# Three expert weight loads, issued from ScalarE's queue at the start of the program

## The chip, the cores and the metric

One core of a Trainium2 chip (trn2) runs the whole program; the seven other cores are idle. The metric is the device time of one execution in microseconds (us). All data is fp32 unless said otherwise. The engines are TensorE (PE), VectorE (DVE), ScalarE (ACT), GpSimd (POOL) and SyncE (SP), each with an instruction queue of its own that it works through in order; 16 DMA engines move the data.

## What is computed

The reference is a "macaron" block over 8 x 512 tokens of width 128 (4096 tokens in all): a mixture-of-experts feed-forward, attention, and the same feed-forward again, with the same weights.

```python
x = x + 0.5 * ffn(layernorm(x), router_w, w_gate, w_up, w_down, ws_gate_up, ws_down)
x = x + attn(layernorm(x), wq, bq, ..., gamma, beta)      # 16 heads of width 8, layernorm inside
x = x + 0.5 * ffn(layernorm(x), ...)

def ffn(x):                       # T = 4096 tokens as given; 64 experts, 8 per token, 64 slots per expert
    probs = softmax(x @ router_w.T)
    topk_w, topk_ids = top_k(probs, 8); topk_w /= sum(topk_w)
    # an expert takes its first 64 tokens, later ones are dropped
    h = silu(xb @ w_gate) * (xb @ w_up)       # per expert: [64,128] @ [128,96], twice
    y = h @ w_down                            # per expert: [64,96] @ [96,128]
    return segment_sum(y * topk_w) + (silu(sg) * su) @ ws_down    # plus one shared expert
```

The three expert weights are `w_gate` and `w_up` [64, 128, 96] and `w_down` [64, 96, 128], each 64 x 128 x 96 x 4 bytes = 3.146 MB, 9.44 MB together. The input tokens are 4096 x 128 x 4 bytes = 2.10 MB.

## The kernel before

The program is one block with a hand-written instruction stream for each engine. Every order between engines is made by semaphores, and `wait(engine, semaphore, count)` holds that engine's queue at this point. Both feed-forwards use the same function `ffn(f)` on each engine, with `f.p` 0 for the first and 1 for the second.

All state stays on chip: `x_sb` holds the 4096 tokens as 32 tiles of 128 tokens, `wg_sb`, `wu_sb` and `wd_sb` hold all expert weights. They are loaded once, and both feed-forwards read them.

The start of the program, in the order of its work:

- SP (lines 322 to 348) issues four loads of 8 token tiles each (L326), the router weight `rw_sb` (L327), two shared-expert weights (L328, L329), the attention's weights and biases (L337 to L347), and then the first third, five DMAs, of the fill of `routed_sums` in HBM with zeros (`zero_sums(0, 0, 3)`, L335). Then it enters `ffn`.
- DVE takes statistics of each tile as the tokens come (L925), waits for the transposed router weight (L927), and computes mean and variance (L659, L661).
- ACT's first instruction is the square root of the variance plus epsilon (L937, in `ffn`), with the load of its table before it; DVE takes the reciprocal (L666). This `rstd` releases everything after it.
- The routing runs over 8 groups of 4 tiles. POOL normalises a group (`normalise`, L503 and L507) into one of two buffers `xn_sb`; it may overwrite a buffer only when SP's store of it into `dispatch_rows` (L355) has landed. PE transposes it (L1064), ACT copies it out of PSUM (L942, L943), PE forms the router's logits (L1069), and DVE takes the 8 best of each token (L688 to L714). SP stores the groups and their weights (L355, L359) and, after the first weights, a second third of the zero fill.
- DVE then makes the list of 64 tokens of each expert in one chain of `max` and `match_replace` (L735, L737), while PE, ACT and POOL compute the shared expert.
- In this time SP issues the last third of the zero fill and then the three expert loads (L374), each counting `s_wexp` up by 16.
- When the list is ready (L752), POOL gathers the rows of two experts per indirect DMA (L550). PE waits for `s_wexp` to be 48 (L1117) and then runs the experts in 16 steps of four (L1125, L1150, L1136); DVE weights the results (L774), POOL adds them into `routed_sums` (L563).

Nothing else reads `s_wexp`, and nothing writes the three weight tiles again. ACT issues no DMA in this kernel.

Of the kernel before, what the change touches and what calls it, by code (L numbers as in the profile page):

```python
# [14 lines left out]
def macaron_kernel(nc, x_in, wq, bq, wk, bk, wv, bv, wo, bo, gamma, beta,  # L15
# [9 lines left out]
    T = B * S  # L25
    NT = T // P
    E, _, F = w_gate.shape
    K8, C = 8, 64
    NP2 = E // 2
# [26 lines left out]
    with ExitStack() as ctx:  # L56
        def sb(name, shape, dt=F32):
            return ctx.enter_context(nc.sbuf_tensor(name, shape, dt))

        def sem(name):  # L60
            return ctx.enter_context(nc.semaphore(name))

        def wait(eng, s, value):

            if isinstance(s, Event):
                s, value = s.sem, value + s.base
            if isinstance(value, int) and value <= 0:
                return
            eng.wait_ge(s, value)
# [30 lines left out]
        wg_sb = sb("wg_sb", [P, E, F])  # L100
        wu_sb = sb("wu_sb", [P, E, F])
        wd_sb = sb("wd_sb", [F, E, D])
# [105 lines left out]
        s_wexp = sem("experts_loaded")  # L208
# [114 lines left out]
        def _(sp):  # L323
# [8 lines left out]
            def zero_sums(p, part=0, parts=1):  # L332
                z = acc_dram[p].rearrange("(c p r) d -> c p (r d)", p=P, r=10)
                for c in range(part, z.shape[0], parts):
                    sp.dma_start(z[c], zeros[:]).then_inc(s_acc0[p], 16)  # L335
# [14 lines left out]
            def ffn(f):  # L350
                rows = xw_dram[f.p].rearrange("(i p) c -> p i c", p=P)

                def store(g, r):
                    wait(sp, f.xn, g + 1)
                    sp.dma_start(rows[:, bass.ds(g * GT, GT), 0:D], xn_sb[:, r, :, :]).then_inc(f.xns[r].sem, 16)  # L355

                def store_w(g, r):
                    wait(sp, f.w, g + 1)
                    sp.dma_start(rows[:, bass.ds(g * GT, GT), D:XW], w_r[r].rearrange("p (i e) -> p i e", i=GT))\  # L359
                      .then_inc(f.ws[r].sem, 16)  # L360
                store(0, 0)
                store(1, 1)
                store_w(0, 0)
                if f.p == 0:
                    zero_sums(0, 1, 3)
                with sp.Fori(1, NG // 2) as i:
                    for r in range(2):
                        store(2 * i + r, r)
                        store_w(2 * i + (r - 1), 1 - r)
                store_w(NG - 1, 1)  # L370
                if f.p == 0:
                    zero_sums(0, 2, 3)
                    for w, t in ((w_gate, wg_sb), (w_up, wu_sb), (w_down, wd_sb)):
                        sp.dma_start(t[:], w.rearrange("e k n -> k e n")).then_inc(s_wexp, 16)  # L374

                wait(sp, f.shx, NG)
                wait(sp, f.sca[0], 16 * (NP2 // 2))
                wait(sp, f.sca[1], 16 * (NP2 // 2))
                accs = acc_dram[f.p].rearrange("(a t) d -> a t d", a=NACC)[:, 0:T, :].rearrange("a (i p) d -> a p i d", p=P)

                def load(g, r):
                    wait(sp, f.acca, g - 1)
                    for a in range(NACC):
                        sp.dma_start(acc_r[r * NACC + a].rearrange("p (i d) -> p i d", i=GT),  # L384
                                     accs[a, :, bass.ds(g * GT, GT), :]).then_inc(f.accl[r].sem, 16)
                def store_out(g):
                    wait(sp, f.acca, g + 1)
                    sp.dma_start(out_rows.rearrange("(i p) d -> p i d", p=P)[:, bass.ds(g * GT, GT), :],
                                 x_sb[:, bass.ds(g * GT, GT), :]).then_inc(s_out, 16)
                load(0, 0)  # L390
                load(1, 1)
                with sp.Fori(1, NG // 2) as i:
                    for r in range(2):
                        load(2 * i + r, r)
                        if f.p == 1:
                            store_out(2 * i + (r - 2))
                if f.p == 1:
                    store_out(NG - 2)
                    store_out(NG - 1)
                    sp.wait_ge(s_out, 16 * NG)  # L400

            def attention():
# [68 lines left out]
                ctx_load(NT - 1, (NT - 1) % NBUF)  # L471

            ffn(ffns[0])
            attention()
            ffn(ffns[1])


# [454 lines left out]

        @block.scalar
        def _(act):
            def ffn(f):
                wait(act, f.ve, 1)
                act.activation(rstd[:], rstd[:], ACT.Sqrt).then_inc(f.sd.sem, 1)  # L937

                def route(g, r):
                    wait(act, f.xtp, g + 1)  # L940
                    wait(act, f.lg, g - 1)
                    act.activation(xT_r[r], bank[r][:], ACT.Copy).then_inc(f.xts.sem, 1)  # L942
                    act.activation(xT_all[:, bass.ds(g * (GT * P), GT * P)], bank[r][:], ACT.Copy).then_inc(f.xts.sem, 1)  # L943
                    wait(act, f.d, GT * (g + 1))
                    wait(act, f.w, g - 1)
                    act.activation(e_r[r], d_r[r], ACT.Exp).then_inc(f.ex.sem, 1)
                route(0, 0)
                route(1, 1)
                with act.Fori(1, NG // 2) as i:
                    for r in range(2):  # L950
                        route(2 * i + r, r)
                for b in range(4):
                    wait(act, f.ktp, b + 1)
                    act.activation(KT[:, b * 512:(b + 1) * 512], bank[4 + b][:], ACT.Copy).then_inc(f.kts.sem, 1)  # L954

                def shared_up(g, r):
                    wait(act, f.shp, g + 1)
                    wait(act, f.shh, g - 1)
                    act.activation(shs[r][0:F, :], bank[r][0:F, :], ACT.Silu).then_inc(f.shs.sem, 1)
                    act.activation(shu[r][0:F, :], bank[2 + r][0:F, :], ACT.Copy).then_inc(f.shc.sem, 1)  # L960

                def shared_out(g, r):
                    wait(act, f.sho, g + 1)
                    wait(act, f.shx, g - 1)
                    act.activation(shy[r], bank[4 + r][:], ACT.Copy, scale=0.5).then_inc(f.shy.sem, 1)
                shared_up(0, 0)
                shared_up(1, 1)
                shared_out(0, 0)
                with act.Fori(1, NG // 2) as i:
                    for r in range(2):  # L970
                        shared_up(2 * i + r, r)
                        shared_out(2 * i + (r - 1), 1 - r)
                shared_out(NG - 1, 1)

                for q in range(NP2 // 2):
                    r = q % 2
                    wait(act, f.gtp, q + 1)
                    wait(act, f.gu, q - 1)
                    act.activation(gT[r], bank[r][:, 0:2 * P], ACT.Copy).then_inc(f.gts.sem, 1)  # L979
                    wait(act, f.gu, q + 1)  # L980
                    wait(act, f.hid, q - 1)
                    act.activation(sil[r][0:F, :], bank[2 + r][0:F, 0:4 * C], ACT.Silu).then_inc(f.sil.sem, 1)  # L982

            def attention():
# [63 lines left out]
                for t in range(NT):  # L1048
                    z = z_sb[:, t * P:(t + 1) * P]
                    act.activation(z, z, ACT.Identity, scale=rstdz[:, t:t + 1], bias=negm[:, t:t + 1]).then_inc(a_zn, 1)  # L1050

            ffn(ffns[0])
            attention()
            ffn(ffns[1])


# [256 lines left out]
```

## Time and profile before

| | us |
|---|---|
| median of 3 runs | 985.01 |
| lowest, highest | 984.28, 988.32 |
| the profiled execution | 990.85 |
| its span, first to last instruction | 989.0 |

| engine | busy us | share of the span |
|---|---|---|
| PE | 681.7 | 69% |
| DVE | 682.7 | 69% |
| ACT | 420.0 | 42% |
| POOL | 409.3 | 41% |

By stage, from the span's start: tokens and statistics until about 15 us, routing until 65 us, the experts' token lists until 108 us, the expert steps until about 210 us, then the sum, attention, and the second feed-forward from 739 us on. In the rows below, SPq is SP's queue: the time of a `DMA_DIRECT2D` there is how long the issuing instruction held the queue, not how long the data took. "Idle before" in brackets is how long the engine had been idle, and what ended it. L12 is line 12 of the kernel.

### The profile page before, as it was taken

Reading aid. Unit: us, or ns where it says so; the run is one execution under the profiler, and the core shown is the slowest. Engines: PE = TensorE matmul, PEld = TensorE weight load, DVE = VectorE, ACT = ScalarE, POOL = GpSimd, SP = SyncE. Lnnn points to the kernel's source line nnn. Section 1 sums busy time; section 2 is a strip of 40 time slices with the busy share of each in tenths; the row PEclk is TensorE's granted clock in tenths of the full one; section 3 lists DMA queues with packets and bytes.
Section 4 is the critical chain, followed back from the end, with each engine's and each line's share of the span. In section 5 each row is a group of like instructions: output and inputs, shape, how many; then the busy total and the mean of one; then the engine's idle time right before and its main releaser. Section 6 shows DMA issues by size and latency. Waiting matters only on the chain.

```text
span 989.0 us, 16170 instructions
## 1 busy us (share of the span) xinstructions
PE 681.7 (69%) x4579; PEld 335.1 (34%) x4579; DVE 682.7 (69%) x1396; ACT 420.0 (42%) x885; POOL 409.3 (41%) x492
## 2 busy tenths in 40 slices
PE   2576397600389999999999999999605682886200
PEld 1443285500123333333333333332104441775100
DVE  5899332358797888888888888887276995322345
ACT  2234011000037777777777777777653350111000
POOL 2417478786622233332223333210045173788722
PEclk9998555555589999999999999999955595555555
DMA  7549733347759964444545444451102200233377
GB/s 233 202 151 292 128 51 52 47 68 207 146 74 253 240 124 91 82 88 91 96 86 93 84 85 89 93 96 34 38 0 70 59 1 23 55 51 53 32 208 216
DMA packets 247426, 103.42 MB, mean 105 GB/s; under 512 B 150713, under 2 KB 238937, under 8 KB 247385
## 3 DMA queue, kind: packets, MB, share of 16 engines
q1 hardware_dynamic: 235096, 92.44, 40.4%
q0 software_dynamic: 12288, 10.49, 7.4%
q8 instruction: 19, 0.31, 0.1%
q14 instruction: 23, 0.18, 0.1%
HBM read 58.33 MB, written 44.30 MB: 104 GB/s over the span
## 4 chain that ended last, share of the span: by engine, by line
PE 42%; DVE 22%; issue 12%; DMA 10%; POOL 6%; ACT 3%; SPq 3%; another core or an unknown queue 1%; DVEq 0%; ACTq 0%; POOLq 0%
PE psum L1223 13%; PE psum L1232 13%; PE psum L1210 10%; DMA routed_sums<-arena 5%; DVE arena L735 4%; DVE arena L737 4%; POOL arena L550 4%; DMA arena<-routed_sums 3%; DVE x_sb L789 2%; ACT arena L1022 2%; DVE arena L835 2%; PE psum L1177 2%; POOL routed_sums L563 1%; SPq L384 1%
## 5 line engine op out<-in xcount | busy, mean ns | idle before, releaser
L835 DVE TENSOR_REDUCE arena<-psum 128x2 f32<-128x1024 f32 x256 | 308.7, 1220 | 51.4 <-PE psum L1210 48.2
L1022 ACT ACTIVATE arena<-psum 128x512 f32<-128x512 f32 x512 | 282.0, 600 | 114.0 <-PE psum L1223 112.6
L1210 PE MATMUL psum<-arena 126*128 126x512 bf16 x512 | 196.8, 391 | 9.7 <-DMA arena<-qk_parts 5.0
L1223 PE MATMUL psum<-arena 128*128 128x512 bf16 x512 | 195.6, 385 | 7.3 <-ACT arena L1022 3.3
L1232 PE MATMUL psum<-arena 128*32 128x512 f32 x1024 | 136.2, 604 | 0.3
L622 POOL CAST arena<-arena 128x256 bf16<-128x256 f32 x32 | 12.7, 398 | 262.6 <-issue 260.1
L774 DVE TENSOR_SCALAR arena<-psum,arena 64x128 f32<-64x128 f32 x128 | 44.7, 350 | 110.2 <-DMA routed_sums<-arena 97.7
L563 POOL DMA_INDIRECT routed_sums<-arena x64 | 101.0, 1578 | 29.3 <-DVE arena L774 15.2
L1223 PEld LDWEIGHTS psum<-arena 128*128 128x128 bf16 x512 | 50.4, 100 | 149.2 <-ACT arena L1022 121.7
L550 POOL DMA_INDIRECT arena<-dispatch_rows,arena x64 | 62.8, 981 | 45.6 <-DVE arena L752 26.7
L789 DVE TENSOR_TENSOR x_sb<-x_sb,arena 128x512 f32<-128x512 f32 (+1 forms) x48 | 48.7, 1015 | 35.9 <-DMA arena<-routed_sums 34.0
L982 ACT ACTIVATE arena<-psum 96x256 f32<-96x256 f32 x32 | 12.2, 381 | 139.1 <-PE psum L1150 124.7
L1210 PEld LDWEIGHTS psum<-arena 126*128 126x128 bf16 x512 | 49.3, 99 | 42.5 <-DVE arena L835 14.8
L1136 PE MATMUL psum<-wd_sb,arena 96*64 96x128 f32 x256 | 35.9, 435 | 34.3 <-DVE arena L759 34.3
L1150 PE MATMUL psum<-arena,wg_sb 128*96 128x64 f32 x256 | 49.4, 374 | 7.6 <-ACT arena L979 5.9
L1069 PE MATMUL psum<-rwT,arena 128*128 128x64 f32 x128 | 31.4, 427 | 29.4 <-ACT arena L942 29.4
L1150 PEld LDWEIGHTS psum<-arena,wg_sb 128*96 128x96 f32 x256 | 43.4, 275 | 18.4 <-issue 10.7
L1150 PE MATMUL psum<-arena,wu_sb 128*96 128x64 f32 x256 | 47.6, 367 | 0.0
L1150 PEld LDWEIGHTS psum<-arena,wu_sb 128*96 128x96 f32 x256 | 44.8, 280 | 0.0
L1172 PE MATMUL psum<-ident,arena 128*128 128x128 f32 x32 | 10.9, 341 | 48.7 <-POOL arena L607 40.5
L1064 PE MATMUL psum<-ident,xn_sb 128*128 128x128 f32 x64 | 17.1, 424 | 37.7 <-POOL xn_sb L507 37.7
L735 DVE MAX8 arena<-arena 128x8 f32<-128x2048 f32 (+1 forms) x32 | 41.3, 1290 | 1.8 <-ACT arena L954 0.8
(120 smaller groups left out, 979.5 us busy)
## 6 DMA issues: line engine op xcount, KB each, us to landing
routed_sums<-zeros SPq DMA_DIRECT2D x26, 640.0 KB, 5.5
arena<-routed_sums SPq DMA_DIRECT2D x64, 256.0 KB, 4.3
arena<-qk_parts SPq DMA_DIRECT2D x128, 96.0 KB
ctx<-arena SPq DMA_DIRECT2D x32, 256.0 KB, 2.0
qk_parts<-arena SPq DMA_DIRECT2D x32, 192.0 KB, 3.7
dispatch_rows<-xn_sb SPq DMA_DIRECT2D x16, 256.0 KB, 2.3
arena<-qk_parts SPq DMA_DIRECT2D x64, 64.0 KB
arena<-ctx SPq DMA_DIRECT2D x64, 64.0 KB, 2.3
```

The costliest lines, as they stand in the source:

```text
L550: pool.indirect_dma_start(out=gat[k % NGB], out_offset=None, in_=xw_dram[f.p], in_offset=bass.IndirectOffsetOnAxis(ap=gidx[:, k:k + 1], ax ...
L563: pool.indirect_dma_start(out=acc_dram[f.p], in_=y_r[k % NYB], in_offset=None, out_offset=bass.IndirectOffsetOnAxis(ap=sidx[:, k:k + 1], a ...
L735: link(dve.max(dst[:, c:c + 8], src))
L737: link(dve.match_replace(src, dst[:, c:c + 8], src, 0.0))
L774: dve.tensor_scalar(y_r[k % NYB][rows, :], bank[4 + r][rows, j * D:(j + 1) * D], gat[k % NGB][rows, col:col + 1], None, ALU.mult).then_inc ...
L789: ins = dve.tensor_tensor(xs, xs, src, ALU.add)
L835: dve.tensor_reduce(mx_r[r % 2][:, 2 * p:2 * p + 2], src, X, ALU.max).then_inc(a_mx, 1)
L1022: act.activation(p_r[tau % NPB], bank[4 + tau % 2][:, :], ACT.Exp, scale=SCALE).then_inc(a_P, 1)
L1150: ins = pe.matmul(bank[2 + r][0:F, off + m * C:off + (m + 1) * C], w[:, 4 * q + m, :], gT[r][:, m * C:(m + 1) * C], start=True, stop=True)
L1210: ins = pe.matmul(bank[tau % 4][:, :], heads(q_st[r], rows, g)[:, qt * P:(qt + 1) * P], heads(k_st[r], rows, g), start=True, stop=True)
L1223: pe.matmul(bank[4 + tau % 2][:, :], keys, heads(q_st[r], rows, g), start=True, stop=True)\
L1232: ins = pe.matmul(bank[6][32 * g:32 * g + 32, :], v_r[r][:, g, kt, :], p_r[(4 * kt + g) % NPB], start=(kt == 0), stop=(kt == 3), tile_posi ...
```

## The change

The three loads leave SP's stream and become the first instructions of ACT's. Tiles, sources, semaphore and counts are the same.

```diff
@@ sync: ffn(f), after store_w(NG - 1, 1) @@
                 if f.p == 0:
                     zero_sums(0, 2, 3)
-                    for w, t in ((w_gate, wg_sb), (w_up, wu_sb), (w_down, wd_sb)):
-                        sp.dma_start(t[:], w.rearrange("e k n -> k e n")).then_inc(s_wexp, 16)
@@ scalar @@
         @block.scalar
         def _(act):
+            for w, t in ((w_gate, wg_sb), (w_up, wu_sb), (w_down, wd_sb)):
+                act.dma_start(t[:], w.rearrange("e k n -> k e n")).then_inc(s_wexp, 16)
+
             def ffn(f):
                 wait(act, f.ve, 1)
```

## Rows read from the trace of the kernel before

**Rows 1.** The timeline, first 19 us: start us, us, engine, line, operation [idle before].

```profile
0.76 1.28 ACT L937 ACT_TABLE_LOAD   x1 [0.76 <-PEq L1303]
0.76 3.71 SPq L326 DMA_DIRECT2D x_sb<-in_L_attn_x  x4
...
10.09 1.65 DVE L925 BATCH_NORM_STATS2 stats<-x_sb 128x6 f32<-128x128 f32 x8 [0.23 <-DMA x_sb<-in_L_attn_x]
...
11.91 2.21 DVE L659 BATCH_NORM_AGGREGATE mv<-stats 128x2 f32<-128x6 f32 x32
...
14.32 3.80 SPq L335 DMA_DIRECT2D routed_sums<-zeros  x5
14.36 0.23 ACT L937 ACTIVATE rstd<-rstd 128x32 f32<-128x32 f32 x1 [12.32 <-DVE rstd L661]
14.62 0.35 DVE L666 RECIPROCAL rstd<-rstd 128x32 f32<-128x32 f32 x1 [0.30 <-ACT rstd L937]
```

**Rows 2.** Timeline of SP's queue, 60 to 100 us, the expert loads.

```profile
69.01 1.04 SPq L374 DMA_DIRECT2D wg_sb<-in_L_ffn_w_gate  x1
70.50 11.91 SPq L374 DMA_DIRECT2D wu_sb<-in_L_ffn_w_up  x1
82.46 9.52 SPq L374 DMA_DIRECT2D wd_sb<-in_L_ffn_w_down  x1
```

**Rows 3.** DMA issues over the span: count, KB each, us from issue to landing.

```profile
wd_sb<-in_L_ffn_w_down SPq DMA_DIRECT2D x1, 3072.0 KB, 30.6
...
wu_sb<-in_L_ffn_w_up SPq DMA_DIRECT2D x1, 0.4 KB, 26.2
```

**Rows 4.** DMA view of 6 to 8 us: tokens alone.

```profile
DMA packets 1166, 0.59 MB, mean 294 GB/s; under 512 B 16, under 2 KB 1166, under 8 KB 1166
## 3 DMA queue, kind: packets, MB, share of 16 engines
q1 hardware_dynamic: 1166, 0.59, 118.4%
```

**Rows 5.** DMA view of 77 to 80 us: gate and up weights alone.

```profile
DMA packets 644, 0.99 MB, mean 330 GB/s; under 512 B 0, under 2 KB 644, under 8 KB 644
```

**Rows 6.** DMA view of 98 to 101 us: down weights alone.

```profile
DMA packets 988, 0.51 MB, mean 169 GB/s; under 512 B 0, under 2 KB 988, under 8 KB 988
```

**Rows 7.** DMA issues between 14 and 20 us: count, KB, us to landing.

```profile
routed_sums<-zeros SPq DMA_DIRECT2D x5, 640.0 KB, 7.8
dispatch_rows<-xn_sb SPq DMA_DIRECT2D x2, 256.0 KB, 8.5
```

**Rows 8.** Chain of waits, 16 to 67 us: start us, us, what.

```profile
18.16 8.72 DMA dispatch_rows<-xn_sb
...
27.27 1.05 POOL xn_sb L503
...
65.35 2.31 DVE arena L735
```

**Rows 9.** The timeline of the second feed-forward, the same stage.

```profile
741.68 0.35 DVE L666 RECIPROCAL rstd<-rstd 128x32 f32<-128x32 f32 x1 [0.30 <-ACT rstd L937]
...
744.36 2.50 SPq L355 DMA_DIRECT2D dispatch_rows<-xn_sb  x2
...
747.01 1.04 POOL L503 TENSOR_TENSOR xn_sb<-x_sb,mv 128x512 f32 x1 [0.56 <-DMA dispatch_rows<-xn_sb]
...
788.32 2.29 DVE L735 MAX8 arena<-arena 128x8 f32<-128x2048 f32 x1 [0.38 <-ACT arena L954]
```

**Rows 10.** The timeline, 108 to 115 us, from the finished list to the first expert matmul.

```profile
108.19 0.19 DVE L752 TENSOR_TENSOR arena<-arena 128x32 uint32<-128x32 f32 x1
...
113.44 0.66 PE L1125 MATMUL psum<-ident,arena 128*128 128x128 f32 x2 [6.73 <-DMA arena<-dispatch_rows,arena]
...
114.57 1.54 PE L1150 MATMUL psum<-arena,wg_sb 128*96 128x64 f32 x8 [0.47 <-ACT arena L979]
```

**Rows 11.** The timeline of the second feed-forward, the same place.

```profile
831.14 0.19 DVE L752 TENSOR_TENSOR arena<-arena 128x32 uint32<-128x32 f32 x1
...
837.21 1.54 PE L1150 MATMUL psum<-arena,wg_sb 128*96 128x64 f32 x8 [0.47 <-ACT arena L979]
```

## The prediction, made blind

> **What bounds the kernel at the two ends of the change.** I read first the chain of waits, to see what the stages around the two places hang on, then the timeline of both places, then the DMA view of short stretches in which one kind of transfer runs alone, and last the same stages of the second feed-forward, which has no expert loads and no zero fill beside it.
>
> At the start everything hangs on the tokens. The last eight statistics begin at 10.09 us, released by the token load; the aggregation follows, ACT takes the square root at 14.36, and `rstd` is ready at 14.62 + 0.35 = 14.97 us [rows 1]. ACT had then been idle for 12.32 us, and before that held only a table load of 1.28 us at 0.76. The 16 DMA engines have nothing to spare while the tokens come: 118.4% by the view's own measure, where packets overlap, at 294 GB/s [rows 4].
>
> The next wait on the path is a DMA again: the store of the first normalised group is issued at 18.16 and POOL gets its buffer back only at 27.27, after 9.11 us, since the five zero fills stand before it in the same queue [rows 1, 7, 8]. In the second feed-forward that step takes 747.01 - 744.36 = 2.65 us [rows 9]. From `rstd` to the first `MAX8` of the lists the first feed-forward needs 65.35 - 14.97 = 50.4 us, the second 788.32 - 742.03 = 46.3 [rows 1, 8, 9]. So some 4.1 us of the first one are owed to this traffic.
>
> At the other end, the expert loads are in flight from 69 us; the last lands at 82.46 + 30.6 = 113.1 us [rows 2, 3]. That looks late, since PE begins at 113.44. But what released PE is the first gather, and from L752 to the first expert matmul it is 114.57 - 108.19 = 6.38 us here and 837.21 - 831.14 = 6.07 us in the second feed-forward, without any load [rows 10, 11].
>
> **What is removed.** Three issues leave SP's queue (22.5 us of it), behind which SP has nothing due until the expert steps are over. The loads leave the stage of the lists, where DVE works from its own tiles. The gain is the difference just read: 0.3 us. It can't be much more, because PE would next wait for the gather, whose time without loads is the 6.07.
>
> **What is added: ACT's queue.** The three issues are copied from SP: 1.04, 11.91 and 9.52 us [rows 2]. The second and third are long because each returns only when the load before it is nearly through: the third returned at 82.46 + 9.52 = 91.98, and the up weights landed at 70.50 + 26.2 = 96.7, 4.7 us later [rows 2, 3]. So ACT is free when gate and up are almost moved. Both are 6.29 MB, at 0.330 MB per us [rows 5] 19.1 us. Beside nothing else ACT would be free about 18 us after the first packet, at some 20 us. The trace has no DMA issued from ACT; I take SP's behaviour for it. The bounds: held for nothing but three short issues (about 3 x 1.04 us, free at 4), or held until everything that shares the engines has passed too (below, 35).
>
> **What is added: the tokens share the engines.** Tokens alone need 2.10 MB / 0.294 = 7.1 us [rows 4]. How two queues divide the engines is not shown, so from both sides. If they take turns by packets: a token packet is 0.59 MB / 1166 = 0.5 KB, 583 pass per us, which is 27 ns on each of 16 engines; a gate or up packet is 0.99 MB / 644 = 1.5 KB, 215 pass per us, 75 ns [rows 4, 5]. One of each takes 102 ns, so 157 token packets pass per us and the 4096 need 26.1 us: 19.0 more. If they take turns by bytes, 4.2 MB at about 0.31 take 13.5 us: 6.4 more. The best case is no delay.
>
> The Trainium skill, "DMA: Bandwidth & Descriptors", section "Queues, rings and completion order", says that each DMA engine goes round its queues by whole packets. No run here has shown it yet; by that rule it is the 26.1 us, by equal bytes the 13.5, and it is one reason for the small chance that I give to the mild case below.
>
> *By packets:* the last tokens come 19.0 us later, and `rstd` at 14.97 + 19.0 = 34.0. In these 26 us gate and up have also passed (26.1 x 157 x 1.5 KB = 6.3 MB), so ACT is free at about 28, and with its table load (1.28, hidden before, now behind the issues) and the square root and reciprocal at 30. The tokens are the later of the two. Delay 19.0 us. SP's small loads follow the tokens in order, so the zero fill stands before the first store again, sharing with the down weights (0.51 MB in 3 us, slow ones [rows 6]); I give back 1 us of the 4.1. Sum: +18.0.
>
> *By bytes:* the tokens are done 6.4 us later and no longer decide. ACT's turn comes after 20 + 7.1 (tokens) = 27, and now SP gets to its five zero fills before that: 3.28 MB, which needed some 8 us [rows 7]. ACT is free at 35, `rstd` is ready at 35 + 1.28 + 0.23 + 0.35 = 37. Delay 22. But the zero fills are through when the first store is issued, so up to 4.1 us come back. Sum: +18.
>
> Both ways of sharing lead to the same place, so I take +18 at the start and -0.3 at the end. Other stages only shift: routing runs at DVE's pace, and the rest of the down weights (some 18 us at 0.169 MB per us [rows 6]) lies beside it with small stores between. The profiled execution would go from 990.85 to about 1008.5, with a span of about 1007. It lies 5.8 us above the median of the runs, and I carry the same difference to the median: 985.0 + 18 = 1003.
>
> **The rivals.**
>
> *The queues hinder each other when issuing.* If the expert issues hold not only ACT but also what turns SP's requests into packets, the four token loads are let in one by one between the expert loads. With the last token load behind all three, the tokens are complete after 19.1 + 3.146 / 0.169 = 18.6 + 7.1 = 44.8 us instead of 7.1: delay 37.7, less the 0.3 and nothing given back, because the zero fill again comes late: 1022. For it: SP's own issues already lengthen when the queue is full (four token issues 3.71 us [rows 1]). Against: nothing in the trace has two issuers of this kind. It decides only if the last token load gets behind the down weights; behind gate and up alone it is 26 us, the forecast. The Trainium skill, "Perfetto Trace Analysis", section "DMA Instruction — HWDGE (DVE, Sync)", says that the descriptor generator is locked for one issuer until it has generated all descriptors. That is this rival, and no row of before can show it.
>
> *The mild case.* ACT is not held, or the engines carry both streams at nearly full rate. Then only the 6.4 us of equal bytes remain, or 20 + 1.9 - 15 = 7 us of ACT. The buffer that comes back at 27.27 regardless [rows 8] hides 2.7 to 4.1 us of that: +3 to +4, 988.5. For it: the loads alone stay below 400 GB/s. Against: the DMA share is over 100% already [rows 4].
>
> *Not slower.* A delay of `rstd` under about 2.7 us disappears wholly in the wait for the zero fill that ends at 27.27. That needs the tokens to be nearly through before expert packets come in numbers, and ACT free before 14 us. Then it is 985.0 - 0.3 = 984.7. It decides at 2.7 us. Against: the first expert issue goes out at 0.76 us, together with the first token issue, and the second and third can't return early unless ACT's queue behaves otherwise than SP's [rows 2].
>
> A real gain has no place: the end of the loads is worth 0.3 us. That the edit does nothing is excluded, since it issues 9.44 MB before the tokens are there.
>
> **How the numbers follow.** Forecast (+14 to +24) 0.62; mutual hindrance 0.20; mild 0.12; not slower 0.06. The likeliest is 1003. The range of 8 in 10: from the mild case at 989, which leaves out the not-slower case and half of the mild one, up to 1024 to hold the hindrance. Of the chance outside, some 0.12 lies below and 0.06 above. One measurement of this kernel tells about 0.5% (4.9 us) from no change. Within it lie the not-slower case and about half of the mild one: same 0.10; faster 0.02; slower 0.88.
>
> **What would show it.** In the profile after: ACT's queue begins with three issues, the second and third over 9 us each, and its table load comes after them, near 28 to 35 us. The last statistics begin near 29 us by packets and near 17 by bytes. `rstd` is ready at 34 to 37. The wait for the first store is shorter than 9.1 us. From L752 to the first expert matmul it is about 6.1 us, and every later stage has its old length. Token statistics beginning after 40 us show the hindrance; ACT's square root before 20 us shows the mild case. I am wrong if ACT's issues are short, if the tokens keep their 10 us, or if later stages change their length.

## The result, and the profile after

| | before | after |
|---|---|---|
| median us | 984.64 (4 runs) | 1007.16 (4 runs) |
| lowest, highest | 983.41, 988.32 | 1005.38, 1008.33 |
| ratio, 95% interval | 1 | 1.0222 (1.0201 to 1.0244) |
| profiled execution | 990.85 | 1005.38 |
| its span | 989.0 | 1003.5 |

The change makes the kernel 22.5 us slower (19.8 to 24.0 by the interval of the ratio); a median of 1003 was forecast. ACT's square root is at line 938 now, DVE's reciprocal at L664, POOL's normalising at L501 and L505, the first `MAX8` of the lists at L733, their end at L750.

The timeline after, its first 32 us and the place where the lists begin (start us, us, engine, line, operation [idle before]):

```profile
0.76 10.10 SPq L326 DMA_DIRECT2D x_sb<-in_L_attn_x  x4
0.81 0.91 ACTq L934 DMA_DIRECT2D wg_sb<-in_L_ffn_w_gate  x1
...
2.18 13.37 ACTq L934 DMA_DIRECT2D wu_sb<-in_L_ffn_w_up  x1
...
15.59 14.54 ACTq L934 DMA_DIRECT2D wd_sb<-in_L_ffn_w_down  x1
15.76 0.76 SPq L328 DMA_DIRECT2D wsgu_sb<-in_L_ffn_ws_gate_up  x1
...
24.21 1.65 DVE L923 BATCH_NORM_STATS2 stats<-x_sb 128x6 f32<-128x128 f32 x8 [2.81 <-DMA x_sb<-in_L_attn_x]
...
28.27 0.18 DVE L659 TENSOR_SCALAR rstd<-mv 128x32 f32<-128x32 f32 x1
30.16 1.28 ACT L938 ACT_TABLE_LOAD   x1 [28.00 <-issue]
31.45 0.23 ACT L938 ACTIVATE rstd<-rstd 128x32 f32<-128x32 f32 x1
31.71 0.35 DVE L664 RECIPROCAL rstd<-rstd 128x32 f32<-128x32 f32 x1 [3.27 <-ACT rstd L938]
...
86.96 2.29 DVE L733 MAX8 arena<-arena 128x8 f32<-128x2048 f32 x1
```

Against [rows 1]: the last statistics begin at 24.21 instead of 10.09. The variance is ready at 28.45, and ACT's table load begins only at 30.16, behind its three issues. `rstd` is ready at 31.71 + 0.35 = 32.06 instead of 14.97: 17.1 us. Of these 14.1 are the tokens and 3.0 what ACT adds, 1.28 of them its table load, which lay hidden before [rows 1].

The two queues beside each other, in the DMA view of 10 to 12 us after:

```profile
DMA packets 618, 0.63 MB, mean 316 GB/s; under 512 B 0, under 2 KB 618, under 8 KB 618
## 3 DMA queue, kind: packets, MB, share of 16 engines
q10 hardware_dynamic: 309, 0.47, 78.1%
q1 hardware_dynamic: 309, 0.16, 30.8%
```

q10 is the new queue, ACT's. Both move 309 packets, ACT's three times as large: here the turn goes by packets. The tokens pass at 155 per us instead of 583 [rows 4].

It doesn't go so all the time. By the same view q1 had moved 1013 packets by 4 us, before q10 came in numbers; from 4 to 6 us q10 moved 406 packets and q1 only 32; from 7 to 16 us they took equal turns; and from 16 to 18 us, when the gate weights were nearly through, q1 moved 992 and q10 only 78.

Then the routing. The chain of waits after:

```profile
34.41 9.06 DMA dispatch_rows<-xn_sb
43.86 1.05 POOL xn_sb L501
...
46.30 13.91 DMA dispatch_rows<-xn_sb
60.55 1.04 POOL xn_sb L501
```

Before, one store was waited for like this, 9.11 us [rows 8]; now there are two: 43.86 - 34.41 = 9.4 and 60.55 - 46.30 = 14.2 us. From `rstd` to the first list step it is 86.96 - 32.06 = 54.9 us instead of 50.4. Together the lists begin 86.96 - 65.35 = 21.6 us later [rows 8]. The timeline after, at the end of the lists:

```profile
129.78 0.19 DVE L750 TENSOR_TENSOR arena<-arena 128x32 uint32<-128x32 f32 x1
...
136.02 1.54 PE L1151 MATMUL psum<-arena,wg_sb 128*96 128x64 f32 x8 [0.47 <-ACT arena L980]
```

That is 6.24 us, 0.14 less than in [rows 10].

From the first expert matmul to the end the profile after needs 867.5 us, and the ten other kernels that were profiled (below) 865.5 to 870.1; so the later stages keep their length. The profiled execution of before is the one that stands out, with 874.4 us: 4.9 of the excess lie between its first expert matmul and its first weighted result (13.0 us, in all the other profiles 8.1), and why is not shown. That is why the spans differ by only 14.5 us and the medians by 22.5. The shift of 21.6 us at the lists is the better measure of the change; less the 0.14 it is 21.5, inside the interval.

### The profile page after: what moved, and what is told of

It reads as the page before. It is cut to its first block, busy times and chain, and to the rows that moved or that the text cites. A ratio compares the mean times of both kernels' runs of the same rounds, so it can differ in the third digit from the quotient of the medians.

```text
span 1003.5 us, 16109 instructions
## 1 busy us (share of the span) xinstructions
PE 676.2 (67%) x4518; PEld 335.1 (33%) x4579; DVE 681.5 (68%) x1396; ACT 420.4 (42%) x887; POOL 408.5 (41%) x492
## 3 DMA queue, kind: packets, MB, share of 16 engines
q10 hardware_dynamic: 10288, 9.44, 3.4%
## 4 chain that ended last, share of the span: by engine, by line
PE 38%; DVE 20%; issue 12%; DMA 11%; POOL 8%; ACT 5%; ACTq 3%; SPq 1%; DVEq 0%; POOLq 0%
PE psum L1233 13%; PE psum L1224 11%; PE psum L1211 9%; DMA routed_sums<-arena 5%; POOL arena L548 5%; ACT arena L1023 4%; DVE arena L733 4%; DVE arena L735 4%; DMA arena<-routed_sums 3%; ACTq L934 3%; DVE x_sb L787 2%; DMA dispatch_rows<-xn_sb 2%; DVE arena L833 2%; POOL routed_sums L561 1%; SPq L382 1%
## 5 line engine op out<-in xcount | busy, mean ns | idle before, releaser
L1224 PE MATMUL psum<-arena 128*128 128x512 bf16 x451 | 172.4, 385 | 7.1 <-ACT arena L1023 3.3
L561 POOL DMA_INDIRECT routed_sums<-arena x64 | 100.9, 1577 | 24.5 <-issue 14.8
L1224 PEld LDWEIGHTS psum<-arena 128*128 128x128 bf16 x512 | 50.4, 100 | 149.1 <-ACT arena L1023 121.7
L548 POOL DMA_INDIRECT arena<-dispatch_rows,arena x64 | 62.6, 977 | 45.0 <-DVE arena L750 26.1
L787 DVE TENSOR_TENSOR x_sb<-x_sb,arena 128x512 f32<-128x512 f32 (+1 forms) x48 | 48.7, 1015 | 33.9 <-DMA arena<-routed_sums 32.1
L1211 PEld LDWEIGHTS psum<-arena 126*128 126x128 bf16 x512 | 49.3, 99 | 42.5 <-DVE arena L833 14.5
L501 POOL TENSOR_TENSOR xn_sb<-x_sb,mv 128x512 f32 (+1 forms) x16 | 17.0, 1065 | 68.3 <-DMA dispatch_rows<-xn_sb 33.8
```

The costliest lines, as they stand in the source:

```text
L548: pool.indirect_dma_start(out=gat[k % NGB], out_offset=None, in_=xw_dram[f.p], in_offset=bass.IndirectOffsetOnAxis(ap=gidx[:, k:k + 1], ax ...
L561: pool.indirect_dma_start(out=acc_dram[f.p], in_=y_r[k % NYB], in_offset=None, out_offset=bass.IndirectOffsetOnAxis(ap=sidx[:, k:k + 1], a ...
L787: ins = dve.tensor_tensor(xs, xs, src, ALU.add)
L1211: ins = pe.matmul(bank[tau % 4][:, :], heads(q_st[r], rows, g)[:, qt * P:(qt + 1) * P], heads(k_st[r], rows, g), start=True, stop=True)
L1224: pe.matmul(bank[4 + tau % 2][:, :], keys, heads(q_st[r], rows, g), start=True, stop=True)\
```

## Experiments

My theory after the result had three terms: the tokens take turns with the expert packets (14.1 us), ACT stands behind its own issues (3.0 us), and the stores of the routing wait longer (4.5 us). The rival for each was that one of the others is the whole cause. "List" is the start of the list steps; the kernel before has 65.35.

| kernel | median us | ratio (95%) | last statistics | `rstd` | first store, us | list |
|---|---|---|---|---|---|---|
| before | 985 | 1 | 10.1 | 15.0 | 9.1 | 65.4 |
| after | 1007.2 | 1.0222 (1.0201 to 1.0244) | 24.2 | 32.1 | 9.4 | 87.0 |
| tokens first | 1013.3 | 1.0289 (1.0275 to 1.0303) | 10.2 | 44.1 | 9.6 | 93.9 |
| gate only | 993.5 | 1.0090 (1.0076 to 1.0104) | 21.1 | 26.1 | 7.4 | 74.3 |
| fill late | 1000.9 | 1.0174 (1.0158 to 1.0190) | 24.1 | 32.0 | 9.4 | 81.3 |
| two ahead | 1000.3 | 1.0156 (1.0142 to 1.0170) | 24.5 | 29.4 | 10.7 | 80.8 |
| down after the square root | 1003.8 | 1.0186 (1.0171 to 1.0201) | 24.5 | 29.4 | 12.0 | 84.0 |
| two ahead, fill late | 994.9 | 1.0095 (1.0080 to 1.0110) | 24.7 | 29.6 | 2.7 | 76.5 |
| fill spread | 984.8 | 0.9995 (0.9983 to 1.0006) | 10.2 | 15.1 | 2.7 | 62.5 |
| fill spread, gate on ACT | 982.8 | 0.9989 (0.9977 to 1.0002) | 10.2 | 15.1 | 2.7 | 63.5 |
| ACT at the old time | 999.4 | 1.0137 (1.0119 to 1.0155) | 10.2 | 15.1 | 9.1 | 65.4 |
| down first | 1011.7 | 1.0278 (1.0263 to 1.0292) | 19.9 | 44.5 | 8.3 | 93.1 |

"First store" runs from the issue of the first store to POOL's next use of a buffer. "Last statistics" is the start of the last eight; for "gate only" it is the middle of a row of sixteen (19.42, 3.43 us long). The ratios are to the runs of before on the same chip (984.4 to 985.0 us). One more kernel was planned, with the square root of the first feed-forward taken by DVE, so that `rstd` doesn't wait for ACT's queue; it gave no time. "Two ahead" and "down after the square root" answer its question.

### Tokens first

```diff
         def _(act):
+            for c in range(4):
+                act.wait_ge(s_x[c], 16)
             for w, t in ((w_gate, wg_sb), (w_up, wu_sb), (w_down, wd_sb)):
                 act.dma_start(...)
```

> ACT waits for all four token loads before it issues the three expert loads, so the tokens have the DMA engines to themselves. Theory 'the issues hold ACT': the tokens land near 10 us as before, but ACT's second and third issue return only when gate and up are nearly moved, near 29 us without the zero fill beside them and 37 us with it; rstd is ready between 31 and 39 us, time 1002 to 1010 us. Theory 'the sharing with the tokens is the whole cost': rstd ready at 15 us, time 985 to 989 us.

The timeline of this kernel:

```profile
10.16 1.64 DVE L923 BATCH_NORM_STATS2 stats<-x_sb 128x6 f32<-128x128 f32 x8 [0.32 <-DMA x_sb<-in_L_attn_x]
...
11.66 13.22 ACTq L936 DMA_DIRECT2D wu_sb<-in_L_ffn_w_up  x1
24.91 17.20 ACTq L936 DMA_DIRECT2D wd_sb<-in_L_ffn_w_down  x1
42.14 1.28 ACT L940 ACT_TABLE_LOAD   x1 [30.51 <-issue]
```

The tokens are undisturbed, and the kernel is slower still: 1013.3, above the range that I had given. ACT is held until 42.1. I had put 37 for this; SP's zero fills, issued from 18.00 us on, now share the engines with these loads. So the hold is a cost of its own, and in the changed kernel it lies almost wholly beneath the late tokens. Taking one cause away there shows the other, in full.

### Gate only

```diff
-            for w, t in ((w_gate, wg_sb), (w_up, wu_sb), (w_down, wd_sb)):
-                act.dma_start(...)
+            act.dma_start(wg_sb[:], ...)          # up and down: SP, old place
```

> Only the gate weights are loaded from ACT at the start; up and down stay on SP at their old place. One issue doesn't hold ACT (0.91 us). Theory 'tokens share by packets': after the first 1000 token packets, 2048 pass one by one beside the 2048 gate packets (13 us), the rest at full rate: last tokens near 18 us instead of 10, rstd near 23 instead of 15, time 992 us. Theory 'only the hold of ACT counts': 985 us. Equal bytes instead of equal packets: rstd near 18, 987 us.

993.5 us, forecast 992. ACT's one issue took 0.89 us and its table load lay hidden again at 1.74. `rstd` came 11.1 us late, through the tokens alone, and the time rose by 9.0. A third of the bytes costs two fifths of the loss. SP's four token issues held its queue for 9.77 us here and 10.10 in the changed kernel (3.71 before), though ACT issues nothing here after 1.7 us: what lengthens them is the traffic, not an issue that ACT has open.

### Fill late

```diff
-            zero_sums(0, 0, 3)          # 5 fills before the first store
...
-                if f.p == 0:
-                    zero_sums(0, 1, 3)  # 4 fills in the routing
...
-                    zero_sums(0, 2, 3)
+                    zero_sums(0)        # all 13 behind the routing
```

> The changed kernel, with all 13 zero fills issued after the routing instead of 5 before and 4 in it. Theory 'the stores stand behind the zero fills in SP's queue': the waits of 9.4 and 12 us for a store shrink to 2 to 4 us, routing takes 46 to 48 us instead of 54.9, time 999 to 1000 us. Theory 'the down weights on the other queue slow the stores': routing stays at 52 us or more, 1004 us or more. The fills then need some 21 us in the 40 us of the lists, which costs nothing.

1000.9 us, and both theories half right: the routing took 81.33 - 32.00 = 49.3 us, between the two. The second wait fell from 14.2 to 50.11 - 46.21 = 3.9 us. The first stayed at 9.4 without any fill in its queue:

```profile
34.35 2.51 SPq L354 DMA_DIRECT2D dispatch_rows<-xn_sb  x2
...
43.76 1.04 POOL L498 TENSOR_TENSOR xn_sb<-x_sb,mv 128x512 f32 x1 [7.32 <-DMA dispatch_rows<-xn_sb]
```

The DMA view of 35 to 40 us of this kernel is

```profile
DMA packets 2006, 1.03 MB, mean 205 GB/s; under 512 B 0, under 2 KB 2006, under 8 KB 2006
## 3 DMA queue, kind: packets, MB, share of 16 engines
q10 hardware_dynamic: 2006, 1.03, 119.8%
```

Not one packet of SP's queue, q1, moved in these five us; only the down weights did. From 41 to 43 us both queues took turns again (634 packets of q1, 638 of q10). So this store joined the turns some 6 us late, while the other queue was in the middle of a load. At the 634 packets in 2 us of those turns, its 512 packets of 0.5 KB would have needed 1.6 us, an estimate from these rows. The 32 token packets from 4 to 6 us in the changed kernel look like the same thing.

### Two ahead

```diff
-            for w, t in ((w_gate, wg_sb), (w_up, wu_sb), (w_down, wd_sb)):
+            for w, t in ((w_gate, wg_sb), (w_up, wu_sb)):       # down: SP, old place
                 act.dma_start(...)
```

> Gate and up stay first on ACT's queue, the down weights go back to SP's old place. The second issue returned at 15.6 us in the changed kernel, so ACT is free long before the tokens are there; these still come at 24 us. Theory 'the third issue adds only the last 3 us of the hold, and down traffic slows the stores of the routing': rstd ready at 29 us instead of 32, the first store waits 3 to 7 us (the zero fill alone), routing 49 to 51 us instead of 54.9; time 997 to 999 us. Theory 'the zero fills alone slow the stores': routing stays near 55 us, time 1003 to 1004 us.

1000.3 us. Its timeline:

```profile
2.18 13.62 ACTq L935 DMA_DIRECT2D wu_sb<-in_L_ffn_w_up  x1
15.84 1.28 ACT L939 ACT_TABLE_LOAD   x1 [13.69 <-issue]
28.74 0.23 ACT L939 ACTIVATE rstd<-rstd 128x32 f32<-128x32 f32 x1 [11.62 <-DVE rstd L660]
```

ACT is free at 15.8, idles 11.6 us, and `rstd` is ready at 29.4, as forecast: the tokens alone give 14.4 us of delay. The first store waited 10.7 us, not 3 to 7: no down load is needed for that wait, the fills are enough. The routing took 51.4 us, and the time is above the 997 to 999 that I had given.

### Down after the square root

```diff
                 act.activation(rstd[:], rstd[:], ACT.Sqrt).then_inc(f.sd.sem, 1)
+                if f.p == 0:
+                    act.dma_start(wd_sb[:], ...)       # gate and up stay first
```

> As the changed kernel, but ACT issues the down weights behind its first square root instead of before it. The down traffic flows at nearly the same time, but rstd doesn't stand behind the issue. Theory 'only the end of the hold is taken away': rstd ready near 29 us instead of 32.1, the store waits stay (9 and 12 us), time 1003 to 1005 us. If the whole delay of rstd were ACT's hold, it would fall by over 10 us. If the tokens alone set it, nothing changes: 1007 us.

1003.8, as the first theory had it: `rstd` 2.6 us sooner, the time 3.3 lower. The third issue is now a row of

```profile
28.82 1.18 ACTq L940 DMA_DIRECT2D wd_sb<-in_L_ffn_w_down  x1
```

The up weights landed at 2.18 + 30.7 = 32.9, and this issue returned at 30.0, as the third issue of the changed kernel had returned at 30.1 with the up weights landing at 33.2. It took 1.18 us instead of 14.54 for the same bytes: what makes it long is the load ahead of it in its queue.

### Two ahead, fill late

The edits of "two ahead" and "fill late" together.

> As f1_two_ahead, with all 13 zero fills behind the routing. With fills late alone the first store still waited 9.4 us, its packets beginning to move only 6 us after its issue, while the down weights were moving. Theory 'what holds the store there is the down load on the other queue': with both gone the first store waits 2.7 us as in the second feed-forward and routing takes 46 to 47 us; time 994 to 996 us. Theory 'something else of the start holds it (small loads, ACT's copies)': the wait stays over 6 us, time 999 us or more. The fills and the down load need 21 + 18 us in the 43 us of the lists and may end a little late: up to 2 us more.

994.9 us. The timeline of this kernel:

```profile
29.23 0.35 DVE L662 RECIPROCAL rstd<-rstd 128x32 f32<-128x32 f32 x1 [0.30 <-ACT rstd L936]
...
31.93 0.40 SPq L354 DMA_DIRECT2D dispatch_rows<-xn_sb  x1
...
34.63 1.04 POOL L499 TENSOR_TENSOR xn_sb<-x_sb,mv 128x512 f32 x1 [0.62 <-DMA dispatch_rows<-xn_sb]
```

The first store now waits 34.63 - 31.93 = 2.7 us, the 2.65 of [rows 9], and the routing takes 76.45 - 29.58 = 46.9 us. Against "fill late" this kernel differs in the down load alone (and in ACT's hold by it), and the first store loses 6.7 us of its wait; against "two ahead" in the fills alone, and it loses 8.0. Either one is enough. The lists still begin 11.1 us late: `rstd` 14.6, through the tokens, less the 3.5 us by which this routing is shorter than before's. The medians differ by 9.9.

### Fill spread

```diff
-            zero_sums(0, 0, 3)
...                                     # in the routing, behind store(g), g = 3 to 7:
+                        if g > 2:
+                            zero_sums(0, chunks=[g - 3])
...
-                    zero_sums(0, 2, 3)
+                    zero_sums(0, chunks=range(NG - 3, 13))    # 8, then the three loads on SP
```

> The kernel before, with the three expert loads where they were, and the zero fill taken away from the first store: none before it, one behind each of the stores from the third group on (five), the remaining eight at the old place ahead of the expert loads. If the 4.1 us that the first routing loses against the second come from the fill in front of the first store, routing takes 46 to 48 us instead of 50.4 and the time is 981 to 983 us, 2 to 4 below the kernel before. If the expert loads, now behind eight fills, land after the first gather, up to 3 us are lost again: 984 us.

984.8 us, no change that can be told: not the 981 to 983 of the gain alone, but the second branch, with late loads. The lists began 2.8 us sooner, but the loads, behind eight fills, came late: the first expert work waited 11.99 us, in the timeline

```profile
115.86 0.69 PE L1129 MATMUL psum<-ident,arena 128*128 128x128 f32 x2 [11.99 <-DMA wd_sb<-in_L_ffn_w_down]
```

From the end of the lists to the first expert matmul it is 117.02 - 105.35 = 11.7 us, 5.3 more than before, where up to 3 were forecast. So the loads at their old place were just in time: the last landed at 113.1, PE began at 113.44 [rows 2, 3, 10].

### Fill spread, gate on ACT

```diff
                 route(0, 0)
                 route(1, 1)
+                if f.p == 0:
+                    act.dma_start(wg_sb[:], ...)      # up and down stay on SP
```

> As f4_fill_spread, with the gate weights issued by ACT after its first two groups of the routing (one issue, which returned in 0.9 us); up and down stay at SP's old place. With the fills spread, the lists began 2.8 us earlier but the first expert matmul 2.5 us later, since the loads landed late. If the gate load fits into the DMA time that routing leaves free, the first expert matmul comes 6.3 us after the end of the lists and the time is 981 to 983 us, 2 to 4 us below the kernel before. If the stores wait for the load on the other queue as they did for the down weights, routing gets 3 to 7 us longer and the time is 985 us or more.

982.8 us, a ratio whose interval still touches 1: at best 0.2% gained. The lists begin at 63.5 and the loads are now in time, 6.2 us from the end of the lists to the first expert matmul. But the gate load was issued at 27.81, and one store beside it, issued at 31.57, was waited for again; from 30 to 34 us q10 moved 818 packets and q1 none:

```profile
41.50 1.24 POOL L507 TENSOR_TENSOR xn_sb<-x_sb,mv 128x512 f32 x1 [9.43 <-DMA dispatch_rows<-xn_sb]
```

It is the lowest median of all, but not shown to beat the kernel before. The store that joined late here shows the same as "fill late", beside another load.

### ACT at the old time

```diff
                 for b in range(4):
                     wait(act, f.ktp, b + 1)
                     act.activation(KT[...], bank[4 + b][:], ACT.Copy)...
+                if f.p == 0:
+                    for w, t in ((w_gate, wg_sb), (w_up, wu_sb), (w_down, wd_sb)):
+                        act.dma_start(...)            # removed from the start
```

> The queue alone is changed, not the time: ACT issues the three loads after its last copy of the keys, near 65 us, where SP had issued them. Theory 'the issues hold the engine that makes them, wherever it is': ACT is held for 22 to 27 us, the shared expert starts near 90 us instead of 65 and ends near 121, behind the lists (108 us); the first expert matmul comes near 123 instead of 114.6, time 992 to 994 us. Theory 'only the time of the loads costs': 985 us.

Against the kernel before the queue differs, and the time of the issues only a little: the gate load goes out at 64.82 instead of 69.01, beside the last zero fills and not behind them. The time is 999.4, well above the 992 to 994 that I gave for the hold. The timeline:

```profile
82.33 9.50 ACTq L956 DMA_DIRECT2D wd_sb<-in_L_ffn_w_down  x1
91.86 1.28 ACT L961 ACT_TABLE_LOAD   x1 [25.74 <-issue]
...
118.57 1.16 PE L1100 MATMUL psum<-wsd_sb,arena 96*128 96x128 f32 x8 [1.81 <-POOL arena L523]
119.66 0.25 PE L1117 MATMUL psum<-ident,arena 64*64 64x64 f32 x1
```

ACT is held from 64.8 to 91.8, 27 us, and the shared expert ends near 120, as forecast. What I had left out is L1117: PE's transpose of the finished list stands behind the shared expert in PE's queue. DVE had its part of the list near 106 and waited for it, so the hold cost 14.3 us at the end of the lists (122.4 instead of 108.2), not the 8 that I had counted at the first expert step.

### Down first

```diff
-            for w, t in ((w_gate, wg_sb), (w_up, wu_sb), (w_down, wd_sb)):
+            for w, t in ((w_down, wd_sb), (w_gate, wg_sb), (w_up, wu_sb)):
```

> The changed kernel with the order down, gate, up. The down packets are as small as the tokens' (0.5 KB), the gate's are three times as large (1.5 KB). Turns by packets: a token packet (27 ns) beside a down packet (27 to 50 ns) leaves 207 to 290 per us instead of 157, so the last statistics begin near 16 to 19 us instead of 24.2. Turns by bytes: near 16 us in both orders, which the changed kernel has already contradicted with 24.2; other causes of the 24.2 (a fixed penalty of the second queue) would leave it at 24. ACT is free only when down and gate have moved, near 36 us, so the time is still above the changed kernel: 1010 to 1015 us.

The DMA view of 10 to 12 us of this kernel:

```profile
DMA packets 1055, 0.53 MB, mean 266 GB/s; under 512 B 16, under 2 KB 1055, under 8 KB 1055
## 3 DMA queue, kind: packets, MB, share of 16 engines
q10 hardware_dynamic: 528, 0.27, 60.7%
q1 hardware_dynamic: 527, 0.26, 59.9%
```

The packets alternate again, 528 to 527, and now that both are small the tokens pass at 264 per us instead of 155. The last statistics begin at 19.9, 4.3 us sooner, a little above the 16 to 19 forecast. The time is 1011.7: ACT was held until 42.5, longer than the 36 that I had put.

## Why the prediction was right, and where it was not

**The direction and the place.** All 21.6 us arise before the lists, through the tokens, ACT's queue and the stores. That the number came so near, 18 for 21.6 at this place, is partly luck. Against the branch by packets the tokens cost 4.9 us less, ACT's queue 3.0 more and the routing 5.5 more, and the errors cancel in part; and since both branches gave +18, the number could not have told them apart.

**The tokens (19.0 by packets, 6.4 by equal bytes).** 14.1 measured. Where both queues move, the turns go by packets (309 to 309, 528 to 527), so the first branch was the right one. Its size was too large because the first quarter of the tokens (1013 packets by 4 us) had passed before expert packets came in numbers, and because another 992 packets passed nearly alone from 16 to 18 us; the near standstill from 4 to 6 us takes some of that back. The last statistics began at 24.2, neither at the 29 nor at the 17 of the two branches.

**ACT's hold (free at 28 or 35).** 30.1 measured. In the branch by packets I had the tokens as the later of the two, by 4 us. It was ACT, by 3.0, and `rstd` came at 32.1, ahead of the 34 to 37 of the forecast. "Tokens first" shows that the hold is a full cost by itself (`rstd` at 44), and "two ahead" and "down after the square root" that without the third issue `rstd` comes 2.7 and 2.6 us sooner. The table load that came out from under the idle time is 1.28 of the 3.0, as forecast.

**The give-back of 1 to 4.1 us in the routing.** This step failed, with its sign: the routing took 4.5 us more. I had laid the whole 4.1 us to the zero fill and took the down weights for harmless neighbours of small stores. The forecast also had the routing run at DVE's pace and the first store wait less than 9.1 us; it waited 9.4. The runs show that either alone makes the first store wait 7.4 to 10.7 us instead of 2.7 ("gate only" and "two ahead" with the fills, "fill late" with the down load), and that in the changed kernel a second store waits 14.2 us behind four fills and the rest of the down load. The measured terms give 17.1 + 4.5 = 21.6 at the lists, beside 22.5 in the medians; the forecast's were 19 to 22 and -1 to -4.

**The end of the loads (0.3).** 0.14 in the profiles. "Fill spread" adds what the forecast didn't say: it is not slack that makes this gain small, since loads that landed at 115.8 instead of 113.1, for lists that ended 2.8 us sooner, cost 5.3 us at once. They were just in time.

**The rivals.** The mutual hindrance, with the last tokens after 40 us, didn't come: fifteen small issues of SP, from 15.76 to 24.9 us, returned in 0.4 to 0.8 us each while ACT's third issue was held. That is of SP's small issues; its token issues were lengthened, and by the traffic ("gate only"). The Trainium skill, "Perfetto Trace Analysis", section "DMA Instruction — HWDGE (DVE, Sync)", has the generator locked for one issuer until its descriptors are made; the trace doesn't agree in that form, since SP issued freely within ACT's 14.54 us. Whether something of it remains where a store's packets begin 6 us late beside a large load ("fill late") is not shown. The Trainium skill, "DMA: Bandwidth & Descriptors", section "Queues, rings and completion order", says turns by whole packets. The trace agrees where both queues move, 309 to 309; the rule alone doesn't account for the stretch from 4 to 6 us, with 32 packets beside 406, or for the stores that join late. The mild case and the not-slower case are excluded by `rstd` at 32.1.

**Open.** Where a new transfer waits for those 6 us is not shown by any view, nor why q10 nearly stopped from 16 to 18 us although the up load's issue had returned at 15.55. And why fills and down load together cost the first store no more than either alone was not tested.

## What to carry to other kernels

A large load on a second queue is not free for the first one: the engines took turns by packets, so the side with the small packets got the smaller share (0.16 MB beside 0.47), and what waited for it started later. An engine that computes was held by its own large issues from the second one on, until the load ahead was nearly through (9.5 to 22.4 us for 3.1 MB); the first issue took 0.5 to 0.9 us, and a third one made late enough 1.18. Move a load earlier only after reading what its landing releases: here that was 0.14 us.

## What was not expected of the hardware

- A store issued while a large load was in flight on the other queue moved no packet for over 5 us (35 to 40 us in "fill late": 2006 packets of q10, none of q1), then took equal turns. "Fill spread, gate on ACT" shows it again, from 30 to 34 us.
- An issue of 3.1 MB took 1.18 us where the load ahead of it was nearly through, and 14.54 or 17.20 us where it was not (the changed kernel, "tokens first").
- Three expert loads, 9.44 MB, and 3.3 MB of zero fill in turns held ACT until 42 us after a start at 10 us in "tokens first", 32 us, where the same three issues took SP 23 us from 69 us on [rows 2].
